# Delta rule: the write keys made by transposes and copies, or by a DMA store and a load one row further down

## What is computed

```python
rk = x / norm(x)                     # read keys, per head, 128 wide
wk = pad(rk[:, :, :-1], one row in front)   # write keys: the read key of the position before
...
def step(S, inp):                    # S: 128 x 128 per batch and head
    v_new = A_i @ vsc_i - A_i @ wkd_i @ S
    o_i = rkd_i @ S + intra_i @ v_new
    S = ced_i * S + wkp_i @ v_new    # wkp: the write keys, transposed
    return S, o_i
```

## Time and profile before

| | us |
|---|---|
| median of 3 runs | 2403.66 |
| lowest and highest run | 2401.52 and 2408.75 |
| the profiled execution, its own time | 2399.99 |
| its span, from the first to the last instruction | 2398.3 |
| the delta rule's chunks, from the first `M2` to POOL's last scatter | 60.2 to 382.3 |

### The profile page before, as it was taken

The page is one execution under the profiler, slowest core; times in us unless marked ns, Lnnn a source line. Parts: engine busy times, 40 slices in busy tenths (PEclk is TensorE's granted clock), DMA queues, the critical chain, the costliest instruction groups (busy, mean ns, idle before and its releaser), DMA issues.

```text
span 2398.3 us, 36952 instructions
## 1 busy us (share of the span) xinstructions
PE 2197.5 (92%) x12464; PEld 1788.7 (75%) x12464; DVE 1843.5 (77%) x2832; ACT 1646.8 (69%) x2715; POOL 1449.4 (60%) x1026
## 2 busy tenths in 40 slices
PE   6799897999999999996999999999999999999986
PEld 4788796998898898884667667676676765776765
DVE  5574453667766666677989989989899899898995
ACT  6775542555555556666887788787877877888774
POOL 0236563111111113336988989889889898898895
PEclk8899998999999999997999999999999999999988
DMA  8434544566666654444655655555555555565563
GB/s 291 85 56 111 112 125 136 181 236 232 234 230 230 233 209 152 133 126 154 219 169 190 198 184 186 194 186 202 176 186 195 199 187 177 185 211 177 178 208 101
DMA packets 235434, 430.22 MB, mean 179 GB/s; under 512 B 35089, under 2 KB 117457, under 8 KB 235234
## 3 DMA queue, kind: packets, MB, share of 16 engines
q1 hardware_dynamic: 229090, 410.87, 53.0%
q0 software_dynamic: 6144, 16.79, 2.2%
HBM read 353.61 MB, written 73.96 MB: 178 GB/s over the span
## 4 chain that ended last, share of the span: by engine, by line
PE 54%; DVE 13%; issue 9%; ACT 9%; DMA 6%; POOL 6%; SPq 1%; another core or an unknown queue 1%; POOLq 1%; DVEq 0%; ACTq 0%
PE pb L1641 11%; PE pb L1614 11%; DVE pb L2094 6%; PE pb L2406 5%; PE pb L2411 5%; PE pb L994 3%; PE pb L2305 2%; PE pb L2432 2%; PE pb L2321 2%; DVE UU L2100 2%; DMA XB<-xnd 2%; PE pb L2330 2%; DMA CC<-bcd 2%; POOL UU L2019 2%; POOL UU L2027 1%
## 5 line engine op out<-in xcount | busy, mean ns | idle before, releaser
L2019 POOL TENSOR_TENSOR UU<-dx,BB 128x1024 f32<-128x1024 f32 x256 | 614.6, 2409 | 112.0 <-DMA BB<-bcd 83.6
L2231 ACT ACTIVATE pb<-dt,al 128x512 f32<-128x512 f32 x512 | 339.5, 685 | 149.4 <-DVE UU L2100 147.8
L2100 DVE TENSOR_TENSOR UU<-pb,CC 128x512 f32<-128x512 f32 x512 | 351.3, 686 | 24.3 <-DMA CC<-bcd 6.5
L2094 DVE TENSOR_TENSOR_SCAN pb<-pb,hs,UU 128x512 f32<-128x512 f32 x256 | 328.5, 1283 | 10.7 <-ACT pb L2231 7.4
L2094 DVE TENSOR_TENSOR_SCAN pb<-pb,UU 128x512 f32<-128x512 f32 x256 | 313.0, 1223 | 8.5 <-ACT pb L2231 7.9
L1381 POOL TENSOR_TENSOR clo_b<-craw_b,chi_b 128x1024 fp32r<-128x1024 f32 x22 | 62.3, 2830 | 405.9 <-ACT chi_b L1444 405.9
L1531 DVE TENSOR_TENSOR HL<-HF,HH 128x512 fp32r<-128x512 f32 x220 | 159.6, 728 | 179.9 <-ACT HH L1436 165.7
L2406 PE MATMUL pb<-HAh,WH 128*128 128x512 f32 x1024 | 282.7, 419 | 7.0 <-DVE dt L2075 5.1
L1431 ACT ACTIVATE HF<-pb,BU 128x512 f32<-128x512 f32 x192 | 132.3, 689 | 219.4 <-PE pb L1614 191.9
L2411 PE MATMUL pb<-HAl,WH 128*128 128x512 f32 x1024 | 259.7, 396 | 0.0
L1641 PE MATMUL pb<-W2h,HH 128*128 128x256 f32 x880 | 256.0, 291 | 1.0
(11 more groups left out here) (336 smaller groups left out, 4891.0 us busy)
## 6 DMA issues: line engine op xcount, KB each, us to landing
WH<-fhd SPq DMA_DIRECT2D x176, 512.0 KB, 3.5
BB<-bcd SPq DMA_DIRECT2D x256, 256.0 KB, 4.7
CC<-bcd SPq DMA_DIRECT2D x256, 256.0 KB, 5.0
raw<-in_w1a SPq DMA_DIRECT2D x23, 1024.0 KB, 7.3
raw<-in_w2a SPq DMA_DIRECT2D x23, 1024.0 KB, 7.4
craw_b<-in_fch SPq DMA_DIRECT2D x22, 512.0 KB, 5.9
fhd<-chi_b SPq DMA_DIRECT2D x22, 512.0 KB, 3.9
fld<-clo_b SPq DMA_DIRECT2D x22, 512.0 KB, 4.9
```

What stands on the lines that cost most here:

```text
L2019: e.tensor_tensor(ubuf(n)[:], dx[p][:], BB[n % 3][:].rearrange("p (a m) -> p a m", a=1).to_broadcast([P, 2, 512]), ALU.mult).then_inc(p_u. ...
L2094: e.tensor_tensor_scan(h_[:], h_[:], uu[:, c, :], first, ALU.mult, ALU.add).then_inc(v_sc.sem, 1)
L2100: e.tensor_tensor(uu[:, c, :], abank(n, c)[:], CC[n % 3][:], ALU.mult).then_inc(v_mu.sem, 1)
L2231: e.activation(abank(n, c)[:], dt[p][:, c, :], ACT.Exp, scale=al1[:, 2 * p + c, s:s + 1]).then_inc(c_a.sem, 1)
```

## The change

In place of the transposes and copies, the read keys go through DRAM. A new DRAM tensor `rkd` holds, for each head and batch, 1025 rows of 128: row 0 is zero, and row t + 1 is the read key of position t. SP stores the tile `rk` of each chunk to rows 1 + 128n and on (`keys_out`, 2 stores of 256 KB), and loads rows 128n and on, one row higher up, to the tile `wk` (`keys_in`, 2 loads of 256 KB). The steps `wkT` on PE and `wk` on ACT are gone. `rows_` on ACT now also waits until the stores of the chunk before have landed, since they read the tile it overwrites. Step `S` on PE waits for the load in place of ACT's copy. The two new semaphores are two that counted loads of x at the start, so their counts begin at 16. One row of zeros per head and batch is stored at the start.

```diff
+        rkd = nc.dram_tensor("rkd", [2, 4, T + 1, P], F32, kind="Internal").ap()
...
-        order = ["kk'", "d4", "wkT", "wkS", "P4", "D4", "P5", "t5", "D5", "rkT''", "t6", "P6", "T6", "MT'", "vn", "v'", "o", "S", "kq'"]
+        order = ["kk'", "d4", "wkS", "P4", "D4", "P5", "t5", "D5", "rkT''", "t6", "P6", "T6", "MT'", "vn", "v'", "o", "S", "kq'"]
...
-                        ["d4", "wk", "rk''", "ETr'", "ET'", "t5", "ez'", "rc'", "rT''", "t6", "MT'", "vn", "Er''", "E''", "o"]) for h in range(2)]
+                        ["d4", "rk''", "ETr'", "ET'", "t5", "ez'", "rc'", "rT''", "t6", "MT'", "vn", "Er''", "E''", "o"]) for h in range(2)]
...
+        s_rkd, s_wk = s_x[6], s_x[7]
...
+            def keys_out(n):
+
+                for h in range(2):
+                    e.wait_ge(*g_act[h].at("rk", n))
+                    e.dma_start(rkd[h, :, 1 + n * P:1 + (n + 1) * P, :].rearrange("b t d -> t b d"), TB[h]["rk"][:]).then_inc(s_rkd, 16)
+
+            def keys_in(n):
+
+                e.wait_ge(s_rkd, 32 + 32 * (n + 1))
+                for h in range(2):
+                    if n:
+                        e.wait_ge(*g_pe[h].at("S", n - 1))
+                    e.dma_start(TB[h]["wk"][:], rkd[h, :, n * P:(n + 1) * P, :].rearrange("b t d -> t b d")).then_inc(s_wk, 16)
+
...
+            e.dma_start(rkd[:, :, 0, :].rearrange("h b d -> (h b) d"), zt[0:8, 0:P]).then_inc(s_rkd, 16)
+            keys_out(0)
             e.wait_ge(*a_dve.at("cumT"))
             e.dma_start(cumd, cumT[:]).then_inc(s_zr, 16)
             e.wait_ge(s_zr, 16)
             blocks(0)
             spread(0)
             sums(1)
+            keys_in(0)
+            keys_out(1)
             zeros(*range(16, NZ))
...
                 if n + 1 < NSEQ:
                     spread(n + 1)
+                if 0 < n < NSEQ - 1:
+                    keys_in(n)
                 if n + 2 < NSEQ:
+                    keys_out(n + 2)
                     sums(n + 2)
...
                         e.wait_ge(*g_pe[h].at("rkT", n - 1))
+                        e.wait_ge(s_rkd, 32 + 32 * n)
...
-                    e.wait_ge(*g_pe[h].at("wkS" if n > 1 else "wkT", n - 1))
+                    e.wait_ge(*(g_pe[h].at("wkS", n - 1) if n > 1 else g_pe[h].at("kq", 0)))
...
-                if more:
-                    copy("wk", n, "wkT", "wk")
...
-                for h in range(2 if more else 0):
-                    turned("wkT", n, h, prev(n, h))
...
-                        e.wait_ge(*g_act[h].at("wk", n))
+                        e.wait_ge(s_wk, 16 + 32 * (n + 1))
                         product("S", n, h, W["wk"], W["vnt"])
```

More of the change, by code:

```diff
@@ L180, in program @@
         r_act = Count(sem("r_act"), ["exp", "p2"])
-        IDLE = {("wkS", 0), ("R", 0), ("S", NSEQ - 1), ("vnt", NSEQ - 1), ("wkT", NSEQ - 1), ("wk", NSEQ - 1)}
+        IDLE = {("wkS", 0), ("R", 0), ("S", NSEQ - 1), ("vnt", NSEQ - 1)}
         class Chunks:
@@ L224, in program @@
             turn.append({k: i for i, k in enumerate(us)})
-        by_act = {"rkT": "rT", "z": "ET", "MT": "MT", "wkT": "wk", "d4": "d4", "o": "o", "t5": "t5", "t6": "t6"}
+        by_act = {"rkT": "rT", "z": "ET", "MT": "MT", "d4": "d4", "o": "o", "t5": "t5", "t6": "t6"}
         by_dve = {"kk": "M", "kq": "iT", "v": "vs", "wkS": "R", "vn": "vnt"}
```

## The result

The change makes the kernel slower. Its median of 8 runs is 2424.89 us (2419.24 to 2428.19), against 2403.22 us of 8 runs of the kernel before on the same chip: ratio 1.0078, 95% interval [1.0059, 1.0096], or +21.7 us. The rival of the clogged queue had put it at 2423.5.

A forecast was written before the change was run, and what follows sets the result against it. Chunks were taken to end with PE, `ZR` through ACT, or POOL's scatters; chunk terms 2.0, 1.0, 0.3, 0 and 2.2 gave +5.5 us on 2399.99, so 2405.5, and 2409.2 us from the median 2403.66; range 2398 to 2424 us.

The forecast's parts named there:

- The rival of the clogged queue: Keys ahead of `ZR` move at the broadcasts' pace, d is 7.8 us: sum 19.8 us, 2423.5 us; chance 0.30.
- What bounds a chunk: Delta rule: a chunk ends with PE, with `ZR` through ACT, or with POOL's scatters.
- The gain: Removed transposes and copies, chunks 0 to 6: 0.9 us in chunk 1 if `ZR` stays hidden, nothing elsewhere; at most 6.1.
- The added waits: `rows_` for the stores, `S` for the load of `wk`, SP for `rk`: cost nothing at these durations.
- has until `S`: The load of `wk`, issued behind `MB`, has until step `S` near the chunk's end, some 10 us: no cost.
- The sum: Chunks 0 to 4 add 2.0, 1.0, 0.3, 0 and 2.2 us, chunks 5 and 6 nothing: +5.5 us.
- the delay d: `ZR` comes 4 us later behind the keys, 2 us in chunk 0; ends 1.9 and 7.8 us.
- the cover in chunk 2: DVE's 2.54 us of idleness before the second `M2` hides 2.5 of `y`'s 2.8 us delay, leaving +0.3.
- The start: Before chunk 0: the added stores go while PE and ACT work on the decays, cost nothing.
- An issue takes about 0.47 us: On SP, from two `ZR` in 0.93 us: four key transfers make `ZR` issue up to 1.9 us later.
- The bound between the cases: Sum goes as 3.5 d - 8.5, so slower by over 7.2 us from d = 4.5 on; 0.33 for that outcome.
- against: the zeros: Argument against the clogged queue: the stores of zeros ended at 281 GB/s, 3.7 us for 1.05 MB.

The follow-up runs named there:

- wide rows: The changed kernel with `rkd` holding the four batches side by side, keys moved in rows of 2 KB, a quarter of the packets: 2418.59 us, ratio 1.0028.
- the first four experiments: Removal with chunk 0's keys alone; transfers added to the kernel before; the change with `ZR` issued first; the change with keys spread: ratios 1.0023, 1.014, 1.0128, 1.0017.
- wide `ZR`: The kernel before with the running sums stored so that `ZR` loads in rows of 2 KB, 128 packets a load: 2396.95 us, ratio 0.9991.

## Why the prediction was right or wrong

- **What bounds a chunk** (`ZR` through ACT and `OT` to `y`): right, and it is through this chain that the loss came. Chunks 3 and 6, where I counted 0, grew 0.6 and 0.0. On the second chip of the experiments chunk 4 grew without it.
- **The gain**: right that it is nothing; the removal alone gives ratios of 1.0023 and 1.0013.
- **The added waits**, `S` for the load of `wk` and `rows_` for the stores: right, at nothing. But "has until `S`" was right for this place only; with `ZR` first the same load is late and costs 1.3%.
- **The sum**, +5.5 us, is the step that failed, in three of its terms; the stage grew by 19.9. Of the 14.4 us between, the delay d was taken too short (4.6 us: 3.6 in chunk 1, 0.7 in chunk 2, 0.3 in chunk 4), a slowed `y` was in no term (4.8 us: 2.2, 0.1 and 2.5), and the cover in chunk 2 did not hold (2.5 us). The start, with +1.8 for 0, is most of the rest.
- **The delay d of `ZR`.** I took 4 us, by the pace of the stores of zeros (281 GB/s), and kept 7.8 as the upper end, by the pace of the broadcasts. Measured were 7.6, 4.7 and 4.3 us in chunks 1, 2 and 4. I reckoned in bytes. Packets count as well: with a quarter of them and the same bytes, chunk 1 grows by 3.3 us in place of 7.4. "An issue takes about 0.47 us" failed with it: behind 2,048 packets the two took up to 5.21 us.
- **The bound between the cases** was named: "slower by over 7.2 us from d = 4.5 on, close to what I take". With ends of 1.9 and 7.8 and this note, the clogged queue deserved more than 0.30; "against: the zeros" compared stores in packets of 0.9 KB (0.56 MB in 626 packets from 82 to 84 us) with transfers in packets of 512 bytes, half of them loads. And the zeros do repeat their source: the code reads one tile `zt` four times for a store.
- **The figures of the Trainium skill** gave an estimate of 2.4 us for d and +1 us in all. The traces show 4.3 to 7.6: full rate at 512 bytes is not what a load behind such rows sees here. With the other rule cited there, ring order, the trace agrees: `ZR` came 4.3 to 7.6 us later behind the keys. A third one of the Trainium skill, DMA: Bandwidth & Descriptors, section "Issuing engines are not separate DMA queues", holds that the time a sequencer needs to start a DMA is usually small against the DMA itself; at 5.21 us for two issues, of 17.2 from issue to use, this is the exception.
- **The slowed `y`**: 2.2 us in chunk 1, 2.5 in chunk 4, at a granted clock of 0.63 in the first, after idle times of 4.60 and 5.37 us. These waits on PE cost more than their length.
- **Chunk 2**: +0.3 forecast, +3.7 measured. I had taken DVE's 2.54 us of idleness as cover. It stood beside POOL's scatters, and these moved too: they begin 33.5 us after the chunk's first store of `M2` in place of 29.1, behind a wait of 4.19 us for `rows`. That the scatters cause the idleness is argued, not shown; if they do, a cover made by work that the same delay moves is none. I had named `rows` as late by d and left that out of the sum.
- **Chunks 0 and 5, and the start**: +1.3 for +2.0. In chunk 5 the -1.8 was met by luck: the forecast had the standstill of 8.95 us shortened and `ZR` free of the keys; in fact the standstill is gone, `ZR` follows the keys at once, takes 4.48 us to issue, and ACT waits 12.54 us for it. Before chunk 0 it is +1.8 for 0: ACT's wait for the first `ZR` grew from 6.46 to 8.14 us, though the keys are issued behind it there. From its issue to its use this `ZR` took 14.1 us in place of 12.6, on the second chip 14.0 in place of 13.4. It looks as if transfers issued behind a load delayed it too, but no experiment tests that.

The rival of the clogged queue came to +19.8 us by d = 7.8 alone; the stage grew by 19.9. That the totals meet is partly luck: its delay was too long in chunks 0, 2 and 4, and the slowed clock and the lost cover, which it did not have, filled the gap.

Left open: why the removal alone is 0.1 to 0.2% slower than nothing; what the rest of the loss with wide rows is; whether two loads ahead of `ZR` would be as harmless as two stores; and what holds DVE and ACT up while POOL scatters (below), which may also be what lengthens chunk 4 on the second chip. The part behind the stage, which the change leaves alone, took 1990 to 2003 us in the profiles of the first four experiments, so differences of 0.2% need not come from the stage. The changed kernel wasn't run on the chip of these four, so the 1.4% of the transfers alone has no ratio of the full change beside it.

## What to carry to other kernels

Before work moves from an engine to a DMA, look at what is issued behind it on the same queue and who waits for that, and count packets as well as bytes: here 2,048 packets ahead of a load that was already waited for cost 0.6 to 0.8%, half as many nothing by the medians, and the same ones in an idle place of the queue nothing more than the removal alone. Look in the trace for an issue that takes longer than its like (6.52 us for four stores that take 1.98 when fewer packets are ahead): it says that the queue holds the issuing engine up already. Ask also what a wait costs beyond its length: the slowed products after the idle gaps were a quarter of the loss here. And before an engine is relieved, find the wait that ends last: PE 5 us earlier was worth 0.6 us in front of POOL's scatters.

## What the runs showed of the hardware

- The issue of a DMA is not free of what is queued: 0.93 us for two `ZR` behind `MB`, 1.28 right behind 1,024 packets more, 4.40 to 5.21 right behind 2,048 more (3.59 to 5.68 in the kernel with the transfers alone), 3.45 when `ZR` comes 1.8 us after them and 1.33 when 3.2 us after, and 1.15 right behind the same bytes in 512 packets.
- The two broadcasts `ZR` to 128 partitions in 512-byte pieces took 11.8 to 14.8 us from issue to use in the kernel before, behind `MB` and with the queue long free, and 16.5 to 18.2 in the change where their issue was held up (chunks 1, 2, 4 and 5); in 2 KB pieces 7.0 to 10.0 us.
- PE's product `y` took 3.6 to 3.7 us after idle times of 1.25, 1.82 and 2.53 us, and 5.78, 6.21 and 5.30 us after 4.60, 5.37 and 7.05, at a granted clock of 0.63 in the first of these and down to 0.54 in the kernel with the transfers alone, which is close to its lower level, 1.2 GHz. The idle time ahead of `y` alone doesn't decide: with the transfers alone it took 6.48 us after 3.15, and with the removal alone, at a granted clock of 0.68, 5.38 after only 2.10 (PE's timeline, chunk 5):

```profile
300.95 5.38 PE L1051 MATMUL pb<-wr,OT 128*128 128x256 f32 x16 [2.10 <-ACT OT L992]
```

- The longest standstills of DVE lie where POOL issues 12 scatters in a row. The place differs from kernel to kernel; before it is 8.95 us in chunk 5, in the kernel with wide `ZR` it comes one chunk earlier and is 12.61 us, though PE's product that DVE reads next had ended 9.8 us before DVE went on. DVE's timeline there:

```profile
249.62 1.13 DVE L718 SCALAR_TENSOR_TENSOR vsc<-pb,sm_bec,vsc 128x128 f32<-128x128 f32 x4 [12.61 <-remote]
```

"remote" is how the profile names a releaser that it can't find. A kernel without the scatters wasn't tried, so their part in this is seen side by side only, not shown.

- The same kernel took 2357.56, 2412.23 and 2400.26 us on the three chips of the experiments and 2403.22 us in the result, 2.3% between the ends and three times what the change itself is worth. Only comparisons on one chip say anything here.
